# Attention scores computed a second time with keys on partitions, in place of transposing the exponentials

## The reference, cut to what matters

```
q   = rope(layernorm(x)[b] @ M1[h])          # 256 queries x 192
qz  = q @ Z[h]                               # 256 queries x 64, in the space of the keys
sim = qz @ rope(ctx[b]).T                    # 256 queries x 256 keys
p   = exp(sim - max over keys);  s = sum of p over keys
ctxt = (p @ rope(ctx[b])) / s                # 256 x 64
out[b] += ctxt @ N[h]                        # 256 x 256, added over the 16 heads
```

## Time and profile before

| | us |
|---|---|
| median of three runs | 621.7 |
| the profiled execution, its own time | 621.75 |
| its span, first to last instruction | 619.5 |
| first L1283 to last L1383 (attention) | 176.9 to 448.2 |
| PE busy | 467.2 (75%) |
| PE weight loads busy | 356.0 (57%) |
| VectorE busy | 429.9 (69%) |
| ScalarE busy | 261.6 (42%) |
| GpSimd busy | 240.9 (39%) |

### The profile page before, as it was taken

One profiled execution on the slowest core, in us unless ns is written; L12 is line 12 of the kernel. 1 busy time (PEld: TensorE's weight loads), 2 busy tenths in 40 slices (PEclk: granted clock), 3 DMA queues, 4 the chain that ended last, 5 costly groups with the idle time before them and its releaser, 6 DMA issues.

```text
span 619.5 us, 11219 instructions
## 1 busy us (share of the span) xinstructions
PE 467.2 (75%) x4270; PEld 356.0 (57%) x4274; DVE 429.9 (69%) x952; ACT 261.6 (42%) x588; POOL 240.9 (39%) x240
## 2 busy tenths in 40 slices
PE   2858438565457999999779978897625999999992
PEld 0547215343345677777567766776412777767782
DVE  3249886999564777788779886887441776767661
ACT  0535434444323455555345533555201555555430
POOL 1077651011132222242153323340232377776765
PEclk9977767788578999999789998999755999999997
DMA  7791390000050000000010501000002255565613
GB/s 207 259 341 25 95 364 5 1 1 0 10 195 1 3 1 1 3 1 2 2 36 2 171 2 36 2 20 1 35 12 85 89 147 136 168 176 172 177 17 42
DMA packets 35331, 47.10 MB, mean 76 GB/s; under 512 B 6608, under 2 KB 30416, under 8 KB 35088
## 3 DMA queue, kind: packets, MB, share of 16 engines
q1 hardware_dynamic: 27856, 40.43, 20.0%
q0 software_dynamic: 3712, 4.79, 4.7%
q10 hardware_dynamic: 3712, 1.18, 0.8%
HBM read 40.56 MB, written 8.55 MB: 79 GB/s over the span
## 4 chain that ended last, share of the span: by engine, by line
PE 40%; DVE 29%; DMA 9%; ACT 7%; POOL 6%; issue 6%; ACTq 3%; SPq 1%; POOLq 0%; DVEq 0%; another core or an unknown queue 0%
PE psum L1283 9%; DMA lw<-dispatch 7%; PE psum L1343 5%; DVE se L948 4%; PE psum L1328 3%; PE psum L1310 3%; PE psum L1357 3%; PE psum L1303 3%; PE psum L1492 3%; PE psum L1506 3%; PE psum L1383 3%; ACT lw L625 2%; ACT lw L598 2%; DVE am L846 2%; DVE lw L836 2%
## 5 line engine op out<-in xcount | busy, mean ns | idle before, releaser
L447 POOL TENSOR_TENSOR lw<-lw 128x512 f32<-128x512 f32 x48 | 60.7, 1269 | 135.8 <-DVE lw L904 135.4
L1283 PE MATMUL psum<-lp 128*128 128x256 f16 x576 | 70.4, 278 | 5.5 <-DVE scat L1017 3.6
L632 ACT ACTIVATE lw<-psum 128x512 f16<-128x512 f32 x64 | 38.2, 597 | 84.5 <-PE psum L1343 84.3
L506 POOL TENSOR_TENSOR lw<-lw 128x320 f16<-128x320 f32 x64 | 50.9, 796 | 46.6 <-DVE lw L1090 45.2
L1506 PE MATMUL psum<-se,lw 128*128 128x256 f16 (+1 forms) x576 | 65.2, 273 | 0.0
L625 ACT ACTIVATE lw<-psum,nmax 128x256 f32<-128x256 f32 x128 | 59.2, 471 | 11.8 <-DVE nmax L915 11.8
L1283 PEld LDWEIGHTS psum<-lp 128*128 128x128 f16 x576 | 55.0, 99 | 14.3 <-DVE scat L1017 3.9
L1506 PEld LDWEIGHTS psum<-se,lw 128*128 128x128 f16 (+1 forms) x576 | 57.2, 102 | 6.3 <-issue 1.7
L693 ACT ACTIVATE lw<-psum,b1w 128x320 f16<-128x320 f32 x64 | 33.7, 527 | 57.7 <-PE psum L1492 57.7
L1492 PE MATMUL psum<-lw,se 128*128 128x320 f16 x384 | 56.6, 307 | 0.7 <-issue 0.7
L920 DVE TENSOR_TENSOR lw<-psum,lw 128x512 f16<-128x512 f32 x64 | 43.8, 684 | 16.1 <-ACT lw L632 14.6
(11 more groups left out here) (197 smaller groups left out, 997.4 us busy)
## 6 DMA issues: line engine op xcount, KB each, us to landing
se<-in_w SPq DMA_DIRECT2D x16, 1024.0 KB, 7.4
dispatch<-in_empty SPq DMA_DIRECT2D x4, 662.5 KB, 9.8
lw<-dispatch SPq DMA_DIRECT2D x8, 265.0 KB, 7.9
lp<-in_Wq SPq DMA_DIRECT2D x1, 2048.0 KB, 14.4
se<-in_WoT SPq DMA_DIRECT2D x1, 2048.0 KB, 16.1
lp<-in_w_kc_q SPq DMA_DIRECT2D x1, 1536.0 KB, 18.5
x_sb<-in_x SPq DMA_DIRECT2D x2, 512.0 KB, 5.8
se<-in_gate_wT SPq DMA_DIRECT2D x1, 1024.0 KB, 9.2
```

Source lines behind the costliest of these rows:

```text
L447: nc.gpsimd.tensor_tensor(rope[:, c % QT, :], t1[:, c % 2, :], t2[:, c % 2, :], ALU.add)\
L506: nc.gpsimd.tensor_tensor(hs[1][:, m, :], hr[:, n % 2, :], hs[0][:, m, :], ALU.subtract)\
L1283: ins = M(tile_bank(c)[:, half * S:(half + 1) * S], m1[w][:, kc, half, col:col + P], (yth, ytl)[a][:, kc, b * S:(b + 1) * S], start=(n == ...
```

## The change

Scores are computed twice. `max_scores` is the old `scores`, now only for the maxima. `turned_scores` computes the same products with the operands exchanged, so that keys lie on partitions, and then adds the negated maximum (now float16) of each query by a product: the weights are the column of maxima read 128 times over, the moving operand is the identity. ScalarE takes one exponential of 128 x 512 per head straight into the orientation that `context` needs. The sums come from a column of ones behind the context (65 columns instead of 64). `at_low` moves from VectorE to GpSimd, with four buffers instead of two. `max_scores` and `turned_scores` rotate over banks 3 to 5. Bank 5 is no longer a transpose bank, a fourth head's context goes to the upper half of bank 1, and all in-loop query tiles use bank 0, one at each of h = 0, 1, 2; `latent(g+2)` stands at h = 3 of the same group. `route_logits` and `route_count` move to bank 2, and some routing steps by one or two n.

```diff
 def tiles_at(n):
-    return [c for c in {2: [QT * (g + 2)], 3: [QT * (g + 2) + 1, QT * (g + 2) + 2]}.get(h, []) if c < QT * NGB]
+    return [c for c in ([QT * (g + 2) + h] if h < QT else []) if c < QT * NGB]
 def tile_bank(c):
-    return bank[(0, 1, 0)[c % QT]]
+    return bank[7] if c < 2 * QT and c % 2 == 1 else bank[0]
+def score_bank(k):
+    return bank[3 + k % 3]
# GpSimd: at_low(0), at_low(1) ahead of the loop, then at_low(n + 2) first in each step, ahead of rotate
+def at_low(n):
+    pool.wait_ge(a_at, n + 1)
+    if n >= 4:
+        pool.wait_ge(p_cx, n - 3)
+    nc.gpsimd.tensor_tensor(at[1][:, n % 4, :], e_sb[:, n % 2, :], at[0][:, n % 4, :], ALU.subtract)\
+        .then_inc(g_at, 1)
# ScalarE: at even n exps(n + 2), exps(n + 3), at_high(n + 2), at_high(n + 3)
 def exps(n):
-    for st in range(TPB):
-        A_(e_sb[:, n % 2, st * S:(st + 1) * S], bank[3 + n % 2][:, st * S:(st + 1) * S], ACT.Exp,
-           bias=nmax[:, n % 2, st:st + 1], accum_out=esum[:, g % 2, st, TURN[h]:TURN[h] + 1]).then_inc(a_exp, 1)
+    A_(e_sb[:, n % 2, :], score_bank(4 * (n // 2) + 2 + n % 2)[:, :], ACT.Exp).then_inc(a_exp, 1)
 def at_high(n):
-    A_(at[0][:, n % 2, :], bank[5][:, :], ACT.Copy).then_inc(a_at, 1)
+    A_(at[0][:, n % 4, :], e_sb[:, n % 2, :], ACT.Copy).then_inc(a_at, 1)
# VectorE
-def at_low(n):
-    V.tensor_tensor(at[1][:, n % 2, :], bank[5][:, :], at[0][:, n % 2, :], ALU.subtract).then_inc(v_at, 1)
 def norm(g):
+    V.reciprocal(rs6, six[:, :, :, DC])
+    link(V.reciprocal(rs[:, 6:8], two[:, :, DC]))
...
+    V.tensor_tensor(o[:, :, 0:3, :], six[:, :, :, 0:DC], rs6.unsqueeze(3).broadcast_to([P, TPB, 3, DC]), ALU.mult)
+    V.tensor_tensor(o[:, :, 3, :], two[:, :, 0:DC], rs[:, 6:8].unsqueeze(2).broadcast_to([P, TPB, DC]),
+                    ALU.mult).then_inc(v_norm, 1)
 for n in range(NHB):
-    if n % 2 == 1 and n + 1 < NHB:
-        maxima(n + 1)
-    at_low(n)
+    if n % 2 == 1 and n + 3 < NHB:
+        maxima(n // 2 + 2)          # both heads of the pair
     if h == 0 and g >= 1:
         norm(g - 1)
     for c in tiles_at(n):
         turn(c)
+    if h == 3 and g + 2 < NGB:
+        qz_low(g + 2)
# TensorE
 def queries(c):
-    if t == 1 and g >= 1:
-        pe.wait_ge(v_qz, g)
-    if t == 0 and c >= 1:
+    if c >= 2 * QT:
         pe.wait_ge(v_t1, c)
+def turned_scores(p):
+    pe.wait_ge(v_max, 2 * p + 2)
+    if p >= 1:
+        pe.wait_ge(a_exp, 2 * p)
+    for lt in range(TPB):
+        for i, (a, w) in enumerate(PASSES):
+            for k in range(2):
+                M(sides[k][:, lt * S:(lt + 1) * S], kvt[w][rows, keys], qz[a][rows, g % 2, cols], ...)
+    for k in range(2):
+        for lt in range(TPB):
+            for st in range(TPB):
+                ins = M(sides[k][:, lt * S + st * P:lt * S + (st + 1) * P],
+                        nmax[:, p % 2, k, st:st + 1].broadcast_to([P, P]), ident16[:, :], ...)
+        ins.then_inc(p_st, 1)
 for n in range(NHB):
-    if n % 2 == 1 and n + 1 < NHB:
-        scores((n + 1) // 2)
-    turn_scores(n)
+    if n % 2 == 0 and n + 2 < NHB:
+        turned_scores(n // 2 + 1)
+    if n % 2 == 1 and n + 3 < NHB:
+        max_scores(n // 2 + 2)
     if n >= 1:
         context(n - 1)
     for c in tiles_at(n):
         queries(c)
-    if h == 1 and g + 1 < NGB:
-        latent(g + 1)
+    if h == 3 and g + 2 < NGB:
+        latent(g + 2)
     if h == 2 and g >= 1:
         turn_context(g - 1)
     if h == 3 and g >= 1:
         project(g - 1)
```

More of the change, by code:

```diff
@@ L101, in program @@
         kvt = [lp([T], F16) for _ in range(2)]
-        kvr = [lp([NT, DC], F16) for _ in range(2)]
+        kvr = [lp([NT, DC + 2], F16) for _ in range(2)]
         lw = sb("lw", [P, 34 * 256])
@@ L143, in program @@
         e_sb = w2([2, 512])
-        at = [w2([2, 512], F16) for _ in range(2)]
+        at_lo = w2([4, 512], F16)
+        at = [raw.bitcast(F16).rearrange("p (a b) -> p a b", a=4), at_lo]
         cxn = w2([512])
         ct = [w2([512], F16) for _ in range(2)]
[L147 to L150, removed]
+        kvdup = raw.rearrange("p (t j d) -> p t j d", t=NT, j=2)
+        nmax = sb("nmax", [P, 2, 2, TPB], F16)
+        rsum = sb("rsum", [P, 2, TPB * G])
         kcos = sb("kcos", [P, TPB, DC])
@@ L481, in _ @@
                     route_rows(b)
-                for b in routed(n, 13):
+                for b in routed(n, 14):
                     route_out(b)
@@ L671, in _ @@
                     split_high((n - 24) // 4)
-                for b in routed(n, 5):
+                for b in routed(n, 7):
                     route_turned(b)
@@ L1018, in route_place @@
                     .then_inc(v_idx, 1)
[L1020 to L1024, removed]
+            for c in range(QT):
+                turn(c)
+            qz_low(0)
+            for c in range(QT, 2 * QT):
+                turn(c)
             maxima(0)
+            qz_low(1)
             maxima(1)
@@ L1314, in latent, with max_scores @@
                 ins.then_inc(p_qz, 1)
-            def scores(p):
+            def max_scores(p):
                 g, pair = p // 2, p % 2
@@ L1409, in route_count @@
                 pe.wait_ge(v_oh, b + 1)
-                pe.wait_ge(v_t1, min(QT * (NG * (b + 1) + 5), QT * NGB))
+                pe.wait_ge(v_qz, min(NG * (b + 1) + 5, NGB))
                 oh2 = ohs[:, :, :].rearrange("p a b -> p (a b)")
                 t0 = TPB * b
-                M(bank[0][:, 0:TPB * NE], trib[:, :], oh2[:, t0 * NE:(t0 + TPB) * NE], start=True, stop=False,
+                M(bank[2][:, 0:TPB * NE], trib[:, :], oh2[:, t0 * NE:(t0 + TPB) * NE], start=True, stop=False,
                   skip_group_check=True)
                 for j in range(t0):
-                    M(bank[0][:, 0:TPB * NE], onesb[:, :], oh2[:, j * NE:(j + TPB) * NE], start=False, stop=False,
+                    M(bank[2][:, 0:TPB * NE], onesb[:, :], oh2[:, j * NE:(j + TPB) * NE], start=False, stop=False,
                       skip_group_check=True)
-                M(bank[0][:, NE:2 * NE], onesb[:, :], oh2[:, 0:NE], start=False, stop=True,
+                M(bank[2][:, NE:2 * NE], onesb[:, :], oh2[:, 0:NE], start=False, stop=True,
                   skip_group_check=True).then_inc(p_pos, 1)
-            for g in range(2):
-                for c in range(QT * g, QT * g + QT):
-                    queries(c)
-                if g == 0:
-                    latent(0)
-            scores(0)
+            for c in range(QT):
+                queries(c)
+            latent(0)
+            for c in range(QT, 2 * QT):
+                queries(c)
+            max_scores(0)
+            latent(1)
+            turned_scores(0)
+            max_scores(1)
             for n in range(NHB):
                 g, h = n // G, n % G
-                if n % 2 == 1 and n + 1 < NHB:
-                    scores((n + 1) // 2)
-                turn_scores(n)
+                if n % 2 == 0 and n + 2 < NHB:
+                    turned_scores(n // 2 + 1)
+                if n % 2 == 1 and n + 3 < NHB:
+                    max_scores(n // 2 + 2)
                 if n >= 1:
                     context(n - 1)
-                for b in routed(n, 6):
+                for b in routed(n, 8):
                     pe.wait_ge(a_yT3, b + 1)
+                for c in tiles_at(n):
+                    queries(c)
+                if h == 3 and g + 2 < NGB:
+                    latent(g + 2)
                 for b in routed(n, 10):
@@ L1441, in _ @@
                     pe.wait_ge(v_idx, b + 1)
-                for c in tiles_at(n):
-                    queries(c)
-                if h == 1 and g + 1 < NGB:
-                    latent(g + 1)
                 if h == 2 and g >= 1:
@@ L1449, in _ @@
                     project(g - 1)
-                for b in routed(n, 5):
+                for b in routed(n, 7):
                     route_turn(b)
-                for b in routed(n, 8):
+                for b in routed(n, 9):
                     route_logits(b)
-                for b in routed(n, 12):
+                for b in routed(n, 13):
                     route_count(b)
```

131 lines of the change are left out of this document (73 added, 58 removed).

## The result

The changed kernel takes 646.99 us (645.66 to 647.74) against 620.05 (617.16 to 622.47) for the kernel before, four runs each: ratio 1.0434, 95% interval 1.0378 to 1.049. It is slower, as forecast, but by 27 us where 8.3 were forecast, more than three times the step, and it lies outside the range of 612 to 643. Its profiled execution has a span of 645.3 us; the one before had 619.5.

What follows compares the result with a forecast made beforehand. TensorE's list plus the exponentials' hole bound the kernel; the ring would replace the hole. First tile at 204.7, loop 229.9 and tail 22 gave 456.6 against 448.25, +8.3 on 621.75: 630 us, range 623 to 637, 8 in 10 within 612 to 643.

Steps and rivals of the forecast that it cites:

- The hole of the exponential: TensorE idle 1.25 us per plain group while ScalarE computes a head's exponentials; forecast to go.
- the ring: Tile, `turn`, next tile, then `rotate` and `latent`: waits of 0.50 and 1.46 us per group, 1.96 together.
- plain period: A group of four heads without routing or other extras: forecast 15.16 us against 14.20 before.
- the list: TensorE's own work per group, one function after another: 12.95 us before, forecast 13.2.
- the tail: Last two groups, without tiles or `latent`, to the last `project`: forecast 22 us.
- The sum for the loop: 14 groups at 15.16 us, 212.2, plus 17.7 of extras: 229.9 against 219.4, so +10.5.
- what stands on top: Loop extras, 17.7 us: routing on TensorE 3.0, `split_low` 4.8, `route_rows` 4.5, `route_pick` 5.4.
- The ends: Before and after the loop: first loop tile starts near 204.7 us, last two groups take 22 us.
- 1: Rival: in routed groups and the last pick the routing stalls dissolve, total 612 us; chance 0.15.
- 2: Rival: half of the routing stalls dissolve, total 621 us, no change that can be told; chance 0.15.
- 3: Rival: TensorE's clock falls behind waits and picks, total 641 us; chance 0.15.
- 4: Rival: repeated column loads slowly in `turned_scores`, a shift product takes 0.109 or 0.15, total 642 to 651 us; chance 0.10.

Runs made afterwards that it cites:

- Experiments 3: Changed kernel with `at_low` moved back from GpSimd to VectorE, behind `turn`: 662.27 us, ratio 1.0648.
- experiment 6: Changed kernel's arithmetic reordered on TensorE (`latent` one step later), pick split, weights' halvings moved, Exp table loaded early, routing steps later: 614.52 us, ratio 0.9899.
- experiment 4: Changed kernel without the eight products that subtract the maximum, so results differ: 636.87 us, ratio 1.024.
- experiment 2: Changed kernel with the four halvings of the experts' weights moved to a group's fourth step: 638.34 us, ratio 1.0244.
- experiment 5: Changed kernel with the weights' halvings in a group's fourth step, Exp table loaded before the first scores, and scatters one step later: 639.08 us, ratio 1.0298.
- experiment 9: experiment 6 plus eight unread products ahead of each of the last five steps and last three TensorE functions: 627.55 us, ratio 1.0056.
- experiment 7: experiment 6 plus GpSimd holding back `at_low` in three steps per routed batch until VectorE's small instructions are done: 608.56 us, ratio 0.9757.
- experiment 8: experiment 2 (changed kernel's own order) plus GpSimd holding back `at_low` in three steps per routed batch: 642.51 us, ratio 1.0291.

## Why the prediction was wrong

**Right: the direction and its mechanism.** The hole of the exponential goes, the ring takes its place, `latent` waits for `rotate` (1.17, forecast as 1.46), the second tile for `turn` (0.21, forecast as 0.50), and a plain period is 15.33 for a forecast of 15.16. Experiments 3, 4 and 6 bear it out: with VectorE loaded more the ring is longer, with less work on it shorter by a part, and with the order changed it is gone. A shift product costs 0.05, forecast 0.061.

**Right by two errors in part: the list.** The busy time, 13.94, can't be set beside the forecast's 13.2 as it stands: a `context` ahead of a wait counts 0.54 there, up to its end, and 0.35 in the forecast, up to where the next function could start. Counted as in the forecast the two waits are 1.35 and 0.40, for 1.46 and 0.50, and the list is 13.6 (15.33 less 1.75). So the list is about 0.4 too short, because I took each function's shortest distance and nothing for the changes between full-row and half-row products, and the waits are 0.2 too long, because on a ring longer work eats the wait behind it. Had the list been the bound, as in experiment 6, the same step would have missed by 0.5 us a group.

**Where the 17 us went.** Attention grew by 22.7 us in the profiled executions, 8.3 were forecast. The largest single miss is the tail, then the halvings, then the plain period. The 14.4 between them are:

- *The sum for the loop*, 237.1 us (208.25 to 445.35) for 229.9: 14 times 0.17 for the period, 2.4, and 4.8 on what stands on top (22.5 for 17.7). Of that the term that was mis-sized is `split_low`: 4.8 forecast, 7.5 by experiment 2. The rest of the extras, 12.9 forecast, is 13.2 there (212.45 less 13 times 15.33). The other 1.8 lie outside those 13 groups: 1.4 ahead of the third `latent`, where the first loop tile runs at a granted clock of 0.50 and takes 2.70 to the next function for 1.41, and 0.4 in a `route_turn` behind the last `latent`. The step that failed in the loop is the sentence that `route_out` delays "only work that has a step to spare". In the changed kernel it doesn't: by way of `at_low` and ScalarE's queue it reaches `split_low`, and in that stretch the sharing with GpSimd, which I had charged to routing alone, and a clock of 0.91 come on top. That halving costs 4.2 where 1.2 was forecast. A second one costs 2.8, since a halving, a `route_norm` and a lower clock add up; the other two cost next to nothing.
- *The ends*, 6.0: the tail took 28.0 us for a forecast of 22, for which I named parts but made no sum. The nearest stretch of the kernel before, 417.27 to 448.25, took 31.0.
- *The ends*, 1.2: group 0's first loop tile. The table of Exp is loaded just ahead of the first exponential, 1.28 us that other work hid before; experiment 5 gets 1.6 back.

The tail's lines in the changed kernel, and the table load:

```profile
201.80 1.28 ACT L639 ACT_TABLE_LOAD   x1
```

```profile
456.94 2.27 POOL L482 TENSOR_TENSOR lw<-lw 128x512 f16<-128x512 f32 x2 [3.73 <-ACT lw L645]
...
459.34 0.81 PE L1395 MATMUL psum<-lp,lw 128*128 128x65 f16 x12 [3.53 <-POOL lw L482]
...
464.39 2.74 PE L1421 MATMUL psum<-lp,lw 128*128 128x256 f16 x12 [0.76 <-DVE lw L957]
```

TensorE is busy 18.7 of 28.0 there and waits 9.2. My 22 had the two `at_low` in a row, for which it waits 3.53, and one slow `project`; the trace has two (2.74 and 2.34 for 1.48), behind waits for `ct_low` and the pick's small instructions that I had no terms for. How the 6 us divide between waits and clock is open; experiment 9 shows only that holding the clock up by added products doesn't pay.

- *Outside attention*, 3.1: 2.4 of them stand at the first query product already (179.3 for 176.9), before anything that the change touches. First products of `latent` in the profiled executions lie anywhere from 185.4 to 190.3 with that part all but unchanged, so the start of attention in one execution against another can differ by up to 5 us with no cause in the change. I had allowed nothing for it.

**The rivals.** 1 and 2, that the routing stalls dissolve: they did not; but in experiment 7 they mostly do (from the second `latent` on no group there is over 15.7 us), once the ring has slack and GpSimd is held back. 3, the clock: it is 0.91, not 1.00, in four groups, behind waits that I had priced too low. 4 is excluded by experiment 4.

## What to carry over

A sum of queue distances gets a ring's steady period right, but the disturbed groups cost more than one term each: follow a delayed instruction through every queue (here scatters, GpSimd, ScalarE, VectorE, TensorE) before calling it covered. When a change moves work off the bound engine and the kernel slows, look for the order and not for the work: the same arithmetic gained 2.4% once each cross-engine result had a step more and GpSimd was kept from running beside VectorE's short serial chain. And before a wait is added to an engine, look whether something behind it in its queue is on the ring: in experiment 8 it was.

## What the runs showed that was not expected

- VectorE's smallest instructions suffer most beside GpSimd. The earlier trace rows had one case, 1.12 us for `gates`. Beside one `at_low` or `rotate` an instruction (or a pair, `wsel`) of 0.17 to 0.26 us took 1.07 to 1.34, and it happens with one tensor as input as well: a copy of 128 x 2 took 1.07, a TENSOR_SCALAR of 128 x 4 with a scalar column 1.19, one of 128 x 2 in experiment 8 1.15. The Trainium skill (SBUF — State Buffer, two separate sides) describes an exclusive lock that one side holds for a whole instruction; the rows agree, and experiment 7 gives a price in a kernel, 19.30 against 14.23 us for a group in which four instructions were 3.9 us longer.
- The same contention works the other way too: an `at_low` that came while `split_low` ran took 2.13 for 1.16 (experiment 2).
- A weight column read 128 times over costs nothing visible: eight such products take 0.62 us from first start to last end, and by experiment 4 one costs 0.05, below the 0.061 that I had put between rows of ordinary weights.
- Each step from products on half the rows to products on all of them put 0.11 us on the next function (experiment 6).
